# Loading the values in two halves, one quarter apart, in a software-pipelined transformer kernel

## The reference

```
x = x + 0.5 * ffn(layernorm(x))      # "first" pass of a sequence
x = x + attn(layernorm(x))           # linear attention, small
x = x + 0.5 * ffn(layernorm(x))      # "second" pass, same weights
```

```
q, k    = x Wq, x Wk                          # per head
v       = sum over experts of mix_v * (x Wv)  # top 2 of 8, sigmoid weights
attn    = softmax(q k / 8) v                  # 256 x 256 scores per head
result  = sum over heads, experts of mask_o * (attn Wo)
```

## Time and profile before

| | |
|---|---|
| median of 3 executions | 2441.39 us (2440.78 to 2442.31) |
| the profiled execution, its own time | 2441.39 us |
| its span in the profile | 2439.6 us |
| TensorE busy (matmul) | 2336.8 us, 96% |
| TensorE busy (weight load, beside it) | 2161.9 us, 89% |
| ScalarE busy | 2078.7 us, 85% |
| VectorE busy | 1913.1 us, 78% |
| GpSimd busy | 1144.3 us, 47% |
| moved by DMA | 388.21 MB, mean 159 GB/s |

### The profile page before, as it was taken

How to read it: one execution, slowest core, us unless ns; L and a number is a source line. 1 busy time by engine, 2 the same in 40 slices (tenths; PEclk the granted TensorE clock), 3 DMA queues, 4 the chain that set the end, 5 groups by cost and what they waited for, 6 DMA issues and landing times.

```text
span 2439.6 us, 120359 instructions
## 1 busy us (share of the span) xinstructions
PE 2336.8 (96%) x49920; PEld 2161.9 (89%) x49920; DVE 1913.1 (78%) x3498; ACT 2078.7 (85%) x6373; POOL 1144.3 (47%) x1126
## 2 busy tenths in 40 slices
PE   3899999999999999999999999999999999999997
PEld 2899989989998999998999999999998999999997
DVE  4787878878877778788788787788887888887874
ACT  3888888888888888888888888888888888888885
POOL 3344545445355455354454454454453553554531
PEclk8999999999999999999999999999999999999998
DMA  3565555556555556556556556555565555555563
GB/s 115 147 173 146 155 157 153 162 156 175 152 166 162 163 152 170 169 152 172 165 153 172 158 163 175 147 171 168 153 172 151 157 169 167 149 169 169 151 184 103
DMA packets 656604, 388.21 MB, mean 159 GB/s; under 512 B 228416, under 2 KB 581568, under 8 KB 656064
## 3 DMA queue, kind: packets, MB, share of 16 engines
q1 hardware_dynamic: 655632, 379.65, 54.2%
q10 hardware_dynamic: 432, 0.85, 0.1%
HBM read 191.64 MB, written 188.74 MB: 156 GB/s over the span
## 4 chain that ended last, share of the span: by engine, by line
PE 88%; ACT 6%; issue 3%; DVE 2%; POOL 1%; DMA 0%; SPq 0%; ACTq 0%; DVEq 0%; POOLq 0%
PE psT L466 19%; PE psS L421 16%; PE psT L483 7%; PE psS L509 7%; PE psT L484 6%; PE psT L485 6%; PE psT L509 6%; PE psT L434 6%; PE psT L478 5%; PE psT L448 5%; ACT PB L780 5%; PE psT L515 1%; DVE QK L719 1%; PE psT L567 1%; DVE NMAX L660 1%
## 5 line engine op out<-in xcount | busy, mean ns | idle before, releaser
L780 ACT ACTIVATE PB<-psS,NMAX 128x256 f32<-128x256 f32 x2048 | 943.4, 488 | 37.1 <-DVE NMAX L660 32.3
L466 PE MATMUL psT<-V,PT 128*64 128x64 f32 x16384 | 547.2, 224 | 23.1 <-issue 22.2
L466 PEld LDWEIGHTS psT<-V,PT 128*64 128x64 f32 x16384 | 507.5, 138 | 52.8 <-issue 27.5
L719 DVE TENSOR_TENSOR QK<-psT,QK 128x512 fp32r<-128x512 f32 x512 | 339.8, 687 | 223.2 <-ACT QK L789 221.6
L421 PE MATMUL psS<-QK 64*128 64x256 f32 x6144 | 477.1, 291 | 0.1
L780 ACT ACTIVATION_READ_ACCUMULATOR PB<-psS,NMAX 128x1 f32 x2048 | 452.7, 221 | 0.0
L421 PEld LDWEIGHTS psS<-QK 64*128 64x128 f32 x6144 | 403.9, 186 | 29.5 <-issue 27.5
L888 POOL TENSOR_TENSOR BT<-MT,diagv 128x1024 f32<-128x1024 f32 x128 | 304.8, 2381 | 243.4 <-DMA MT<-MIXd 243.4
L660 DVE TENSOR_REDUCE NMAX<-psS 128x2 f32<-128x512 f32 x512 | 329.4, 685 | 97.2 <-PE psS L421 93.9
L789 ACT ACTIVATE QK<-psT 128x512 fp32r<-128x512 f32 x512 | 297.9, 622 | 116.7 <-PE psT L485 102.5
L869 ACT ACTIVATE PT<-psS 128x512 f32<-128x512 f32 x512 | 280.4, 605 | 47.5 <-PE psS L509 43.6
(11 more groups left out here) (119 smaller groups left out, 4539.3 us busy)
## 6 DMA issues: line engine op xcount, KB each, us to landing
Vd<-VM SPq DMA_DIRECT2D x512, 128.0 KB, 2.3
V<-Vd SPq DMA_DIRECT2D x256, 256.0 KB, 4.0
AOd<-AO SPq DMA_DIRECT2D x256, 256.0 KB, 4.0
AR<-AOd SPq DMA_DIRECT2D x256, 256.0 KB, 4.2
PJd<-PJ SPq DMA_DIRECT2D x64, 512.0 KB, 4.0
PR<-PJd SPq DMA_DIRECT2D x256, 128.0 KB, 2.4
MIXd<-MIX SPq DMA_DIRECT2D x64, 128.0 KB, 2.4
MT<-MIXd SPq DMA_DIRECT2D x64, 128.0 KB, 4.8
```

Of the source, the lines that this page charges most:

```text
L466: last = eng.matmul(M[64 * u:64 * u + 64, (t * NT + it) * DH:(t * NT + it + 1) * DH], PT[:, t, jt, cols], V[:, pm % 2, 4 * r + t, jt, :], ...
L719: eng.tensor_tensor(QK[:, 1, ab], bank("qk", m).rearrange("p (k t) -> p k t", k=2), QK[:, 0, ab].bitcast(F32), ALU.subtract).then_inc(free ...
L780: eng.activation(PB[:, ab, j, it, :], psS[:, ab, j, it, :], ACT.Exp, bias=NMAX[:, ab, j, it:it + 1], accum_out=SUM[:, p % 2, it, 4 * r + t ...
```

## The change

It has four parts, all but one in SyncE's program.

1. `load_values` takes a half. Its second half (partitions 64 to 127) is issued at r = 0 of pass p, where the whole load was. Its first half (partitions 0 to 63) is issued one quarter earlier, at r = 3 of pass p - 1, ahead of the `PR` load. Each waits only for the store of its own half. There are now eight loads of half the size in place of four.
2. The wait at r = 3 for `product(n - 1)`, which stood ahead of the `PR` load, is gone.
3. The store of `PJ` at r = 2 moves from behind `store_values(p + 1, 0)` and the `AO` store to a place ahead of both.
4. TensorE's wait in front of `product(4p)` is for 32 instead of 16 per part, because eight DMAs signal now.

```diff
-            def load_values(q):
+            def load_values(q, half):
+                rows = slice(64 * half, 64 * half + 64)
                 eng.wait_ge(s_split, 4)
-                for half in range(2):
-                    eng.wait_ge(s_vw[half], 16 * PARTS * (q + 1))
+                eng.wait_ge(s_vw[half], 16 * PARTS * (q + 1))
                 wait_full(eng, "product", 4 * (q - 2) + 3)
-                loaded = V[:, q % 2].rearrange("p h n d -> p (h n d)")
-                stored = Vd[q % 2].rearrange("(p x) -> p x", p=P)
+                loaded = V[rows, q % 2].rearrange("p h n d -> p (h n d)")
+                stored = Vd[q % 2].rearrange("(p x) -> p x", p=P)[rows]
...
                 if r == 0 and runs(p):
-                    load_values(p)
+                    load_values(p, 1)
...
+                if r == 2 and runs(p + 2):
+                    q = p + 2
+                    wait_freed(eng, "expert", q, 0)
+                    wait_freed(eng, "expert", q, 1)
+                    if q >= 2:
+                        eng.wait_ge(s_pr, 16 * PARTS * (q - 1))
+                    eng.dma_start(PJd[q % 2].rearrange("(p x) -> p x", p=P),
+                                  PJ[:, :, :, :].rearrange("p e n d -> p (e n d)")).then_inc(s_pjw, 16)
                 if r == 2 and runs(p + 1):
                     store_values(p + 1, 0)
-                if r == 3:
-                    wait_full(eng, "product", n - 1)
+                if r == 3 and runs(p + 1):
+                    load_values(p + 1, 0)
                 if r == 3 and runs(p + 2):
                     q = p + 2
                     eng.wait_ge(s_pjw, 16 * (q + 1))
...
-                if r == 2 and runs(p + 2):
-                    q = p + 2
-                    wait_freed(eng, "expert", q, 0)
...
                 if r == 0:
-                    eng.wait_ge(s_value[pm % 2], 16 * PARTS * (pm // 2 + 1))
+                    eng.wait_ge(s_value[pm % 2], 32 * PARTS * (pm // 2 + 1))
```

## The result

The changed kernel is slower: 2453.14 us median (2451.96 to 2456.58), the kernel before 2441.09 on the same chip, ratio 1.0057, 95% interval [1.0043, 1.0072]. The ratio rests on more executions than the two medians, ten of the changed kernel, and so isn't their quotient (1.0049). The forecast was 2435.0, faster.

The account below looks back on a forecast made before the run. TensorE was taken as the bound, 88% of the span. Terms -2.5 - 2.4 - 1.2 = -6.1 us, plus -0.3 for a lighter burst at r = 0, gave 2441.4 - 6.4 = 2435.0; own range 2432 to 2438, whole range 2428 to 2447.

Parts of the forecast that it names:

- The 62 other passes: All passes but 0 and 1: V isn't late there, so nothing to win but side effects.
- The PJ store, and the wait for the product taken out: At r = 2 and r = 3: PJ store and PR load go earlier, neither on TensorE's path; gain 0, no loss visible.
- rival B: TensorE's stops inside product groups lengthen as PJ's 0.5 MB follows the AR load: 2465 us, or 2450 with half; chance 0.17.
- Four more issues a pass: SyncE's four extra V issues at r = 3 fall in a waiting gap: 0, bounds 0 and 1.8 us at p = 0.
- V at pass 0: First product of pass 0 starts at 64.35 instead of 66.86, half of V landing sooner: -2.5 us, bounds -4.2 and 0.
- rival A: Hardly any gain: half load takes as long as the whole, or the clock falls anyway; about 2438.5 us, chance 0.27.
- The clock at pass 0: TensorE resumes before the clock's fall at about 65.5 us, so full speed is kept: -2.4 us, bounds 0 and -2.5.
- pass 1's wait: TensorE's 1.16 us idle before pass 1's first product goes, half of V coming sooner: -1.2 us, bounds 0 and -1.2.

Follow-up runs that it names:

- the gate: An added wait: GpSimd's first BT spread of a pass waits until VectorE has done L625 of r = 0; on the kernel before 2432.92 us, 0.9999.
- wait_back: The changed kernel with the wait for product(n - 1) at r = 3 put back ahead of the PR load: 2455.85 us, ratio 1.0081.
- gate_bt: The changed kernel with GpSimd's first BT spread of a pass waiting for VectorE's L625 of r = 0: 2444.08 us, ratio 1.0032 to the kernel before.
- pj_only: The kernel before with only the PJ store moved ahead of the Vd and AO stores at r = 2: 2453.65 us, ratio 1.0067.

## Why the prediction was wrong

**The 62 other passes: "nothing in the other 62 but side effects", costed at 0.** This is the step that failed, and the side effects were the result: +14.7 us in 50 passes. I followed V and what SyncE issues ahead of it, and not what is queued behind it. MT is, and GpSimd was waiting for it: the waits of the BT spread for MT were 243 us in total before and 142 after. A GpSimd engine that is busy 47% of the time looks free, but a VectorE operation with two inputs in SBUF that begins inside its 2.4 us spread is held to the end of it, and MT's lateness had kept them apart. Of the 14.7 us, the gate gives back 10.9 (1862.7 to 1851.8) in one profile each; by the ratios it is 0.25 of 0.57%.

**The PJ store, and the wait for the product taken out: "Gain 0. Nor is a loss visible".** Wrong on both. The wait taken out is the one good part, -0.31% alone. The store is +0.67% alone, as rival B described it, but in full only while the wait stands: in the changed kernel, without the wait, the stops of class 0 are 7.3 us, against 7.7 before; with the wait back (wait_back) they are 16.1. So B, to which I gave 0.17, had the right kind of loss and the wrong transfer. The stops did become longer in the changed kernel, by V's first half and not by the PJ store. The parts don't add: 0.83 + 0.67 - 0.31 is 1.19%, measured 0.57%.

**Four more issues a pass, costed at 0.** Their issue time stayed hidden (no product of a whole group waits in passes 10 to 59), though an issue is dearer than I took it (below). But the moment of the first half's data was not free: +8.8 us of stops in passes 4k + 3, and with the gate a pass of class 3 is still 0.46 us longer (36.90 against 36.44). I had looked for a gap in SyncE's queue, and had named TensorE's stops, but only for the PJ store.

**V at pass 0: -2.5 us was far too large.** The product starts at 66.39 instead of 66.86, 0.5 us earlier. I had 0.8 us from an earlier issue and 1.7 from a shorter move. The head after, first and second half of V in SyncE's queue, then TensorE:

```profile
51.77 2.38 SPq L324 DMA_DIRECT2D V<-Vd  x4
...
61.10 2.38 SPq L324 DMA_DIRECT2D V<-Vd  x4
```

```profile
62.13 2.88 PE L421 MATMUL psS<-QK 64*128 64x256 f32 x24
66.39 2.08 PE L466 MATMUL psT<-V,PT 128*64 128x64 f32 x64 [1.37 <-issue]
```

From issue to product half of V takes 66.39 - 61.10 = 5.29 us, the whole took 6.05; I had 4.35. The issue itself came 0.3 us later than before, not 0.8 earlier. The stretch in which the half moved:

```profile
65.00:66.00 1.00, 0.01 (x1) 0.00 (x0) 1.00 (x2) 1.00 (x7) 0.00 (x0) 1.00 1.11 179
```

The DMA engines are full, 1.11, at 179 GB/s, where the whole V moved 324 at 1.10. The Trainium skill's rule that I had cited (SBUF — State Buffer, the section on the DMA port swizzle), 8 of the 16 ports for 64 partitions and 196 GB/s, agrees with the 179. At that rate the half moves in some 2.9 us, an estimate, and I had 2.75. So most of the missing 0.94 us lies outside the moving: 0.62 of it in the four issues, which took 2.38 us where I had 1.76. At 5.29 us the half load lies about halfway between my term and rival A, in which it takes as long as the whole.

**The clock at pass 0.** It was at 1.00 from 65 us on, nearly as I had said, and the product took 2.08 us. But it had been at 0.50 before, from 62 to 64 us, and the scores took 2.88 us for 1.75: time was lost in another place. The wait of 1.37 us is short in part because these scores ended late. With pass 1's wait gone, as forecast, the head's gain is 3.8 us instead of 6.1.

Nor can these 3.8 us be laid to the split. In gate_bt, whose SyncE program is the same, the product of pass 0 waits 3.60 us, the clock is at 0.50 from 66 to 68 us, and pass 1's first product starts at 100.08. In pj_only, with V whole, V's load goes out at 57.73 instead of 60.81, and that product starts at 97.29. So the earlier PJ store alone can win as much in the head, and kernels with the same V loads differ there by 2.3 us, with the granted clock low at different moments.

**What stays open.** Why the wait for the product, taken out alone, shortens the stops of class 0, and why with it gone the PJ store costs less, is not settled: PR and Vd move earlier, but no run shows which of them matters. That late blocks of instructions are what TensorE waits for is inferred: the stops move with the instruction stream and lengthen with DMA traffic, but no row shows a block arriving.

## What to carry to other kernels

When a transfer is made shorter or earlier, list what is queued behind it and who waits for that: the consumer that gets its data sooner may start on top of another engine's operation and hold it up. An engine's low busy share doesn't make its operations harmless to a neighbour; compare the neighbour's busy time at an equal count of instructions. In a kernel bound by TensorE to 98%, differences of half a per cent may come from the places of such stops in its instruction stream: a run with some instructions added that do nothing tells how much of a gain comes from there.

## What the runs showed of the hardware

- VectorE operations with two inputs in SBUF wait for a GpSimd operation that has begun, until it ends: L739 2.46 us against 0.29, L625 up to 2.63 against 0.42 (bf16), L621 up to 2.84 against 0.68. Those that read PSUM kept their times: 51 of L660 begin inside a BT spread in the changed kernel, and none takes over 0.69 us. Nor does any of the 40 of L719 that do, and L719 has one input in PSUM and one in SBUF.
- V's halves, 128 KB to 64 partitions, take longer to issue than its whole pieces, 256 KB to 128: the median is 590 ns against 432.
- While they move with the DMA engines full, V's halves reach 179 GB/s and the whole pieces 324.
- 128 waits at the start of TensorE's program, met at once, made the kernel before 0.52% faster.
- The stops come in steps. Over all runs the lengths in front of the last 22 are 0.17, 0.44, 0.72, 0.99, 1.27 and 1.54 us (within 0.01 but for one of 141), 0.27 to 0.28 apart.
- Two stops of 3.03 us were each followed by 3.4 us at a granted clock of 0.50 (pj_only).
